# Moving VectorE's gate/up subtraction one tile ahead in a sparse-expert stage

## The chip, the cores and the metric

One core of a Trainium2 chip. The metric is the device time of one execution in microseconds, the median of the runs shown; lower is better.

## The reference

Four sequences of 2048 tokens of width 512 pass through two residual layers. The first is a selective state-space layer (layer norm, convolution over 4 taps, projection, scan, output projection). The second, where the change lies, is a mixture of 64 experts with 8 chosen per token, cut here to what matters:

```python
idx_flat = topk_idx.reshape(-1)
sort = jnp.argsort(idx_flat)
x_sorted = x_flat[sort // TOPK]
g = jax.lax.ragged_dot(x_sorted, we_gate, group_sizes)
u = jax.lax.ragged_dot(x_sorted, we_up, group_sizes)
o = jax.lax.ragged_dot(jax.nn.silu(g) * u, we_down, group_sizes)
y = jnp.zeros_like(x_flat).at[sort // TOPK].add(o * w_sorted[:, None])
```

Gate and up are 512x256 per expert, down is 256x512, all in float32. 8192 tokens times 8 experts are 65536 rows.

## The kernel before

The program runs in stages: the state-space layer's inputs, its scan, a pass over token blocks (router, shared expert), a table of tiles, and last `expert_tiles`, which is about four fifths of the time and the only stage that the change touches. It works on 576 tiles of up to 128 rows, sorted by expert. A float32 product is made as three products of numbers cut to a high and a low part: high times high, high of x times low of w, low of x times high of w.

Five engines each walk the tiles in an order written out by hand, and wait for each other on semaphores only.

- **SyncE** (`load_weights`, lines 1480 to 1491) runs six tiles ahead: it waits until the subtraction of the down part of an earlier tile has freed a half of `w_raw` (`w_low_ready[1]`), then issues gate, up and down, on the condition that the tile's weights are new. `w_raw` has two halves, `w_high` and `w_low` have four slots each. `retire` waits for an add to `out` to land.
- **GpSimd** gathers x of the tile five ahead (L1518) and adds the result of the tile two behind to `out` (L1526), the latter only when the tiles that it shares tokens with are retired.
- **TensorE**, step i: turns x of tile i+1 (`turn_x`, L1562), which waits until VectorE has taken x of tile i; at i = 1 modulo 4 searches the next four tiles' tokens (`find`, L1574); gate/up of tile i (L1592, twelve products into one PSUM bank), with register reads between the products (`read_ahead`, line 1624, most of them at i = 0 modulo 4); turns h of tile i-1 (L1621); down of tile i-2 (L1611). `turn_h` waits for VectorE's low part of the h before it.
- **ScalarE**, step i: takes the high part of x of tile i+1 (L1678), copies ids and weight, casts the high part of new gate/up weights for tile **i+2** (`split_high` part 0, L1670) and of new down weights for tile i+1 (part 1), silu of tile i (L1689), high part of h of tile i-1 (L1694).
- **VectorE**, step i (`step`, lines 1784 to 1800): reads register words of the tiles that it will need (`words.load`, whose instructions have line 1446), takes the low part of x of tile i+1 (`keep_low`, L1741, the "take"), subtracts new gate/up weights of tile i+1 (`split_low` part 0, L1733), subtracts new down weights of tile i (part 1, L1733 too), at i = 2 and 3 modulo 4 picks tokens (`pick`, L1772 to L1781), at i = 2 modulo 4 marks (`mark`, L1765), makes silu times up of tile i (`hidden`, L1753, the inner product's input), takes the low part of h of tile i-1 (`keep_h_low`, L1747) and scales the output of tile i-2 (`scale`, L1760).

`split_low` waits for ScalarE's cast of that part, branches on whether the tile's weights are new, and in either case drains the engine and counts up. Its queue runs in order, so what stands behind a wait or a drain waits as well. VectorE's loop holds four steps; because registers don't pass from one turn of the loop to the next in the program's text, the step at i = 0 modulo 4 loads the words that the other steps have from their forerunners.

Of the kernel before, what the change touches and what calls it, by code (L numbers as in the profile page):

```python
# [33 lines left out]
UNROLL, SHORT = 8, 4  # L34
# [7 lines left out]
def after(eng, sem, count):  # L42

    if not isinstance(count, int) or count > 0:
        eng.wait_ge(sem, count)
# [1297 lines left out]
def expert_tiles(nc, k):  # L1343
# [8 lines left out]
    with ExitStack() as ctx:  # L1352
# [89 lines left out]
        def exists(i):  # L1442
            return not isinstance(i, int) or 0 <= i < TILES
# [26 lines left out]
        def split_weights(eng, words, s, move):  # L1470

            half = eng.snap(words.place(s) & 1)
            with eng.If(words.is_new(s)):
                move(half, words.place(s))
# [252 lines left out]
        def _(v):  # L1727
            words = Words(v)

            def split_low(i, s, part):  # L1730
                v.wait_ge(w_high_ready[part], i + 1)
                v.sem_inc(dve_begun, 1)
                split_weights(v, words, s, lambda half, place: nc.vector.tensor_tensor(  # L1733
                    w_low[:, bass.ds(place, 1), PARTS[part]], w_raw[:, bass.ds(half, 1), PARTS[part]],
                    w_high[:, bass.ds(place, 1), PARTS[part]].bitcast(F32), ALU.subtract))
                v.drain().then_inc(w_low_ready[part], 1)  # L1736

            def keep_low(i, s):
                v.wait_ge(xT_high_ready, i + 1)
                after(v, gu_done, i - 1)  # L1740
                nc.vector.tensor_tensor(xT_low[:, s % 2], ps_x[:], xT_high[:, s % 2].bitcast(F32),  # L1741
                                        ALU.subtract).then_inc(xT_low_ready, 1)

            def keep_h_low(i, s):
                v.wait_ge(hT_high_ready, i + 1)
                after(v, y_done, i - 1)
                nc.vector.tensor_tensor(hT_low[:, s % 2], ps_h[:], hT_high[:, s % 2].bitcast(F32),  # L1747
                                        ALU.subtract).then_inc(hT_low_ready, 1)

            def hidden(i, s):  # L1750
                v.wait_ge(silu_ready, i + 1)
                after(v, ht_done, i - 1)
                nc.vector.tensor_tensor(h[:, s % 2, :], silu[:, s % 2, :], ps_gu[s % 2][:, 1, :],  # L1753
                                        ALU.mult).then_inc(h_made, 1)

            def scale(i, s, slot):
                v.wait_ge(y_done, i + 1)
                v.wait_ge(weight_ready, i + 1)
                after(v, retired, i - YS + 2)
                nc.vector.tensor_scalar(y[:, bass.ds(slot, 1), :].rearrange("p o d -> p (o d)"), ps_y[s % 2][:],  # L1760
                                        weight[:, bass.ds(slot, 1)], None, ALU.mult).then_inc(y_made, 1)

            def mark(i):

                nc.vector.tensor_tensor(past[:], k.slot_row[:].unsqueeze(1).to_broadcast([NB, SHORT, P]),  # L1765
                                        k.begin[:, bass.ds(i, SHORT)].unsqueeze(2).to_broadcast([NB, SHORT, P]),
                                        ALU.is_ge).then_inc(marked, SHORT)

            def pick(i, t):

                v.wait_ge(found, i + t + 2)
                nc.vector.tensor_tensor(rest[:, t:t + 2], k.rank[:, bass.ds(i + t, 2)], ps_find[t // 2][:, :, P],  # L1772
                                        ALU.subtract)
                v.drain()
                for u in range(2):
                    nc.vector.scalar_tensor_tensor(out=below[:, u], in0=ps_find[t // 2][:, u, 0:P],  # L1776
                                                   scalar=rest[:, t + u:t + u + 1], in1=k.last_weight[:],
                                                   op0=ALU.is_le, op1=ALU.mult,
                                                   accum_out=tokens[:, t + u:t + u + 1])
                v.drain()  # L1780
                nc.vector.tensor_tensor(tile_ids[:, bass.ds(i + t, 2)], tokens[:, t:t + 2], ps_find[t // 2][:, :, P + 1],  # L1781
                                        ALU.add).then_inc(picked, 2)

            def step(i, s, slot):
                if s == 0:
                    words.load(i, s)
                words.load(i + 1, (s + 1) % SHORT)
                if exists(i + 1):
                    keep_low(i + 1, (s + 1) % SHORT)
                    split_low(i + 1, (s + 1) % SHORT, 0)  # L1790
                split_low(i, s, 1)
                if s in (2, 3) and exists(i - s + AHEAD_FIND):
                    pick(i - s + AHEAD_FIND, 2 * s - 4)
                if s == 2 and exists(i - s + SHORT + AHEAD_FIND):
                    mark(i - s + SHORT + AHEAD_FIND)
                hidden(i, s)
                if exists(i - 1):
                    keep_h_low(i - 1, (s - 1) % SHORT)
                if exists(i - 2):
                    scale(i - 2, (s - 2) % SHORT, slot(UNROLL - 2))  # L1800
# [4 lines left out]
                pick(i, 0)  # L1805
                pick(i, 2)
            mark(AHEAD_FIND)
            words.load(0, 0)
            split_low(0, 0, 0)
            keep_low(0, 0)  # L1810
            short_walk(v, step)
            keep_h_low(TILES - 1, SHORT - 1)
            for i in (2, 1):
# [103 lines left out]
```

## Time and profile before

| what | value |
|---|---|
| median of 3 runs | 3840.3 us (3835.18 to 3843.41) |
| the profiled execution | 3837.43 us |
| its span | 3835.7 us |
| TensorE busy with matmuls | 3532.6 us (92%) |
| VectorE busy | 2327.1 us (61%) |
| ScalarE busy | 1360.8 us (35%) |
| GpSimd busy | 1736.8 us (45%) |
| mean granted TensorE clock | 0.971 of full speed |

Times of the profile are counted from the first instruction. A busy share is that of the engine's own work: register, branch, semaphore and drain instructions are not in it, though they take their time in the engine's queue. L and a number is a line of the kernel; "<-" behind an idle time names what ended it, and "issue" stands for nothing that the profile shows, often the engine's own queue.

### The profile page before, as it was taken

The numbers are of one execution on the slowest core, as the hardware profiler recorded it, in microseconds if no ns is written. First come the engines' busy times: TensorE is split into PE (matmuls) and PEld (weight loads), VectorE is DVE, ScalarE is ACT, GpSimd is POOL, SyncE is SP. The second block draws the span as 40 slices with busy tenths as digits, with TensorE's granted clock in tenths as the row PEclk, the third lists the DMA queues.
The fourth block names the chain that finished last, engine by engine and source line by source line (L and its number), as shares of the span: only waits on it lengthen the run. The fifth ranks groups of instructions, "written<-read, shape, count | busy, mean of one in ns | idle before, by whom it ended". The sixth has DMA issues, their size and how long they took to land.

```text
span 3835.7 us, 109938 instructions
## 1 busy us (share of the span) xinstructions
PE 3532.6 (92%) x17240; PEld 2862.0 (75%) x17241; DVE 2327.1 (61%) x5877; ACT 1360.8 (35%) x4103; POOL 1736.8 (45%) x1372
## 2 busy tenths in 40 slices
PE   5929988769999999999999999999999999999996
PEld 3517777648787788787888788888887878888885
DVE  5457777655656566666565656566556566566653
ACT  2233333223334333343333433333333343333331
POOL 1011111125555555555555555555555555555543
PEclk9969999879999999999999999999999999999998
DMA  3323333336667666676666766666666667667654
GB/s 125 104 80 110 120 111 109 81 81 127 154 141 170 140 156 124 141 171 157 126 123 130 185 114 139 142 143 138 127 143 123 140 155 174 138 127 168 129 99 74
DMA packets 217551, 502.59 MB, mean 131 GB/s; under 512 B 47504, under 2 KB 47632, under 8 KB 217114
## 3 DMA queue, kind: packets, MB, share of 16 engines
q0 software_dynamic: 129024, 320.94, 43.4%
q1 hardware_dynamic: 87130, 176.22, 13.9%
q10 hardware_dynamic: 1344, 4.85, 0.4%
q8 instruction: 18, 0.29, 0.0%
q14 instruction: 35, 0.29, 0.0%
HBM read 1115.79 MB, written 191.41 MB: 341 GB/s over the span
## 4 chain that ended last, share of the span: by engine, by line
PE 67%; issue 4%; DMA 3%; DVE 2%; DVEq 1%; ACT 1%; ACTq 0%; POOLq 0%; SPq 0%; POOL 0%
PE e_ps_gu L1592 38%; PE e_ps_y L1611 19%; PE e_ps_x L1562 6%; PE e_ps_h L1621 3%; DMA out<-e_y,e_y_ids 3%; PE e_ps_find L1574 1%; DVE e_w_low L1733 1%; DVEq L1446 1%; DMA e_w_raw<-in_L_ffn_we_down 0%; DVE e_below L1776 0%; ACT e_w_high L1670 0%; DVE e_xT_low L1741 0%; DVEq L1736 0%; ACT e_xT_high L1678 0%; DVE e_y L1760 0%
## 5 line engine op out<-in xcount | busy, mean ns | idle before, releaser
L1526 POOL DMA_INDIRECT out<-e_y,e_y_ids x576 | 994.4, 1726 | 1231.8 <-SPq L1496 601.9
L1592 PE MATMUL e_ps_gu<-e_w_high,e_xT_high 128*128 x2304 | 689.0, 419 | 31.2 <-issue 25.8
L1518 POOL DMA_INDIRECT e_x<-token_rows,e_x_ids x576 | 619.7, 1076 | 212.8 <-issue 169.9
L1592 PE MATMUL e_ps_gu<-e_w_high,e_xT_low 128*128 x2304 | 636.2, 398 | 0.0
L1592 PE MATMUL e_ps_gu<-e_w_low,e_xT_high 128*128 x2304 | 635.7, 398 | 0.0
L1689 ACT ACTIVATE e_silu<-e_ps_gu 128x256 f32<-128x256 f32 x576 | 222.2, 386 | 1018.7 <-PE e_ps_gu L1592 994.2
L1760 DVE TENSOR_SCALAR e_y<-e_ps_y,e_weight 128x512 f32 (+1 forms) x576 | 430.0, 746 | 236.2 <-PE e_ps_y L1611 223.6
L1741 DVE TENSOR_TENSOR e_xT_low<-e_ps_x,e_xT_high 128x512 fp32r<-128x512 f32 x576 | 397.2, 690 | 265.1 <-ACT e_xT_high L1678 126.8
L1592 PEld LDWEIGHTS e_ps_gu<-e_w_high,e_xT_low 128*128 128x128 f32 x2304 | 436.1, 189 | 107.1
L1592 PEld LDWEIGHTS e_ps_gu<-e_w_low,e_xT_high 128*128 128x128 f32 x2304 | 435.2, 189 | 102.6
L1592 PEld LDWEIGHTS e_ps_gu<-e_w_high,e_xT_high 128*128 128x128 f32 x2304 | 396.9, 192 | 111.3 <-issue 48.9
L1753 DVE TENSOR_TENSOR e_h<-e_silu,e_ps_gu 128x256 f32<-128x256 f32 x576 | 240.1, 417 | 384.7 <-ACT e_silu L1689 348.5
L1678 ACT CAST e_xT_high<-e_ps_x 128x512 fp32r<-128x512 f32 x576 | 337.0, 585 | 336.8 <-PE e_ps_x L1562 335.7
L1562 PEld LDWEIGHTS e_ps_x<-ident,e_x 128*128 128x128 f32 x2304 | 365.3, 204 | 66.4 <-DVE e_xT_low L1741 10.3
L1611 PE MATMUL e_ps_y<-e_w_high,e_hT_high 128*128 x1152 | 412.3, 438 | 0.0
L1562 PE MATMUL e_ps_x<-ident,e_x 128*128 128x128 f32 x2304 | 367.6, 282 | 12.1 <-DVE e_xT_low L1741 10.0
L1611 PE MATMUL e_ps_y<-e_w_high,e_hT_low 128*128 x1152 | 363.0, 396 | 0.0
L1611 PE MATMUL e_ps_y<-e_w_low,e_hT_high 128*128 x1152 | 362.8, 396 | 0.0
L1698 ACT CAST e_x_ids<-e_tile_ids (+1 forms) x576 | 110.1, 192 | 499.3 <-issue 382.8
L1621 PEld LDWEIGHTS e_ps_h<-ident,e_h 128*128 128x128 f32 x1152 | 225.4, 197 | 58.2 <-DVE e_h L1753 8.7
L1611 PEld LDWEIGHTS e_ps_y<-e_w_high,e_hT_low 128*128 128x128 f32 x1152 | 218.4, 190 | 51.1
L1611 PEld LDWEIGHTS e_ps_y<-e_w_low,e_hT_high 128*128 128x128 f32 x1152 | 216.7, 188 | 52.7
(292 smaller groups left out, 4140.4 us busy)
## 6 DMA issues: line engine op xcount, KB each, us to landing
e_w_raw<-in_L_ffn_we_gate SPq DMA_DIRECT2D x576, 512.0 KB
e_w_raw<-in_L_ffn_we_up SPq DMA_DIRECT2D x576, 512.0 KB
e_w_raw<-in_L_ffn_we_down SPq DMA_DIRECT2D x576, 512.0 KB
a_x<-in_L_attn_x SPq DMA_DIRECT2D x64, 256.0 KB, 3.8
t_x_in<-in_L_attn_x SPq DMA_DIRECT2D x64, 256.0 KB, 2.7
token_rows<-t_xn SPq DMA_DIRECT2D x64, 256.0 KB, 2.0
out<-t_y_out SPq DMA_DIRECT2D x64, 256.0 KB, 2.1
e_x<-token_rows,e_x_ids POOLq DMA_INDIRECT x576
```

The source lines that it names most:

```text
L1518: pool.indirect_dma_start(x[:, s % XS, :], None, k.rows, bass.IndirectOffsetOnAxis(x_ids[:, s:s + 1], 0)) \
L1526: pool.indirect_dma_start(k.out, bass.IndirectOffsetOnAxis(y_ids[:, s:s + 1], 0), y[:, s % YS, :], None, compute_op=ALU.add).then_inc(adde ...
L1562: last = nc.tensor.transpose(ps_x[:, c, :], chunks[:, c, :], k.ident[:])
L1592: last = nc.tensor.matmul(ps_gu[s % 2][:], x[:, s % 2, c, :], w[:, c], start=(n == 0), stop=(n == 3 * DC - 1))
L1611: last = nc.tensor.matmul(ps_y[s % 2][:], x[:, s % 2, c, :], w[:, c], start=(n == 0), stop=(n == 3 * FC - 1))
L1621: last = nc.tensor.transpose(ps_h[:, c, :], chunks[:, c, :], k.ident[:])
L1678: nc.scalar.copy(xT_high[:, s % 2], ps_x[:]).then_inc(xT_high_ready, 1)
L1689: nc.scalar.activation(silu[:, s % 2, :], ps_gu[s % 2][:, 0, :], ACT.Silu).then_inc(silu_ready, 1)
L1698: nc.scalar.copy(x_ids[:, bass.ds(column, 1)], tile_ids[:, bass.ds(i, 1)]).then_inc(ids_ready, 1)
L1741: nc.vector.tensor_tensor(xT_low[:, s % 2], ps_x[:], xT_high[:, s % 2].bitcast(F32), ALU.subtract).then_inc(xT_low_ready, 1)
L1753: nc.vector.tensor_tensor(h[:, s % 2, :], silu[:, s % 2, :], ps_gu[s % 2][:, 1, :], ALU.mult).then_inc(h_made, 1)
L1760: nc.vector.tensor_scalar(y[:, bass.ds(slot, 1), :].rearrange("p o d -> p (o d)"), ps_y[s % 2][:], weight[:, bass.ds(slot, 1)], None, ALU. ...
```

## The change

In VectorE's walk the subtraction of new gate/up weights is made for tile i+2 instead of i+1, and stands behind the subtraction of the down part, the picks and the mark, directly in front of the inner product. The register words are loaded for i+2 in every step, and at i = 0 modulo 4 for i and i+1 as well. In front of the loop, the subtraction is made for tiles 0 and 1.

```diff
             def step(i, s, slot):
                 if s == 0:
                     words.load(i, s)
-                words.load(i + 1, (s + 1) % SHORT)
+                    words.load(i + 1, s + 1)
+                words.load(i + 2, (s + 2) % SHORT)
                 if exists(i + 1):
                     keep_low(i + 1, (s + 1) % SHORT)
-                    split_low(i + 1, (s + 1) % SHORT, 0)
                 split_low(i, s, 1)
                 if s in (2, 3) and exists(i - s + AHEAD_FIND):
                     pick(i - s + AHEAD_FIND, 2 * s - 4)
                 if s == 2 and exists(i - s + SHORT + AHEAD_FIND):
                     mark(i - s + SHORT + AHEAD_FIND)
+                if exists(i + 2):
+                    split_low(i + 2, (s + 2) % SHORT, 0)
                 hidden(i, s)
...
             mark(AHEAD_FIND)
-            words.load(0, 0)
-            split_low(0, 0, 0)
+            for i in range(2):
+                words.load(i, i)
+                split_low(i, i, 0)
             keep_low(0, 0)
             short_walk(v, step)
```

## Rows read from the trace of the kernel before

**Rows 1.** The page: its first line, and the chain that ended last, by line.

```profile
span 3835.7 us, 109938 instructions
...
PE e_ps_gu L1592 38%; PE e_ps_y L1611 19%; PE e_ps_x L1562 6%; PE e_ps_h L1621 3%; DMA out<-e_y,e_y_ids 3%; PE e_ps_find L1574 1%; DVE e_w_low L1733 1%; DVEq L1446 1%; DMA e_w_raw<-in_L_ffn_we_down 0%; DVE e_below L1776 0%; ACT e_w_high L1670 0%; DVE e_xT_low L1741 0%; DVEq L1736 0%; ACT e_xT_high L1678 0%; DVE e_y L1760 0%
```

**Rows 2.** Timeline, first gate/up products of tiles 0, 229, 233, 540: start us, us, what.

```profile
812.96 1.63 PE L1592 MATMUL e_ps_gu<-e_w_high,e_xT_high 128*128 x3
...
2000.87 0.97 PE L1592 MATMUL e_ps_gu<-e_w_high,e_xT_high 128*128 x3
...
2021.06 1.20 PE L1592 MATMUL e_ps_gu<-e_w_high,e_xT_high 128*128 x4
...
3615.13 1.17 PE L1592 MATMUL e_ps_gu<-e_w_high,e_xT_high 128*128 x4
```

**Rows 3.** Chain of waits in order of time, from tile 542's output: start, us, what.

```profile
3648.02 4.83 DMA out<-e_y,e_y_ids
```

**Rows 4.** Instructions of line 1733: count, duration ns (min/median/max), first and last start.

```profile
L1733 DVE TENSOR_TENSOR e_w_low<-e_w_raw,e_w_high x128: 1224/1749/2349, 809.0 to 3608.4; - x128
```

**Rows 5.** Quiet step of tile 52: timeline, and line 1446 in that step and in all.

```profile
1079.22 1.17 PE L1592 MATMUL e_ps_gu<-e_w_high,e_xT_high 128*128 x4
...
1081.30 0.69 DVE L1741 TENSOR_TENSOR e_xT_low<-e_ps_x,e_xT_high 128x512 fp32r<-128x512 f32 x1 [1.27 <-ACT e_xT_high L1678]
1081.49 1.91 ACT L1670 CAST e_w_high<-e_w_raw  x1 [0.44 <-issue]
...
1084.64 0.73 PE L1592 MATMUL e_ps_gu<-e_w_high,e_xT_high 128*128 x2
...
L1446 DVEq TENSOR_LOAD <-tiles x2: 308/310/311, 1079.8 to 1080.5; - x2
...
L1446 DVEq TENSOR_LOAD <-tiles x720: 300/311/1152, 807.4 to 3787.0; - x180
```

**Rows 6.** Timeline: step of tile 108.

```profile
1372.87 1.17 PE L1592 MATMUL e_ps_gu<-e_w_high,e_xT_high 128*128 x4
...
1375.70 0.69 DVE L1741 TENSOR_TENSOR e_xT_low<-e_ps_x,e_xT_high 128x512 fp32r<-128x512 f32 x1 [1.06 <-issue]
...
1378.30 0.96 PE L1592 MATMUL e_ps_gu<-e_w_high,e_xT_high 128*128 x3
```

**Rows 7.** Timeline: step of tile 60, which has new weights.

```profile
1121.21 1.17 PE L1592 MATMUL e_ps_gu<-e_w_high,e_xT_high 128*128 x4
...
1124.51 0.69 DVE L1741 TENSOR_TENSOR e_xT_low<-e_ps_x,e_xT_high 128x512 fp32r<-128x512 f32 x1 [1.05 <-PE e_ps_gu L1592]
...
1127.11 1.20 PE L1592 MATMUL e_ps_gu<-e_w_high,e_xT_high 128*128 x4 [0.21 <-ACT e_xT_high L1678]
```

**Rows 8.** Timeline: steps of tile 43, which has new weights, and 44.

```profile
1032.29 1.17 PE L1592 MATMUL e_ps_gu<-e_w_high,e_xT_high 128*128 x4
...
1035.22 0.67 DVE L1741 TENSOR_TENSOR e_xT_low<-e_ps_x,e_xT_high 128x512 fp32r<-128x512 f32 x1
...
1037.21 1.17 PE L1592 MATMUL e_ps_gu<-e_w_high,e_xT_high 128*128 x4
...
1041.68 0.69 DVE L1741 TENSOR_TENSOR e_xT_low<-e_ps_x,e_xT_high 128x512 fp32r<-128x512 f32 x1 [1.05 <-issue]
...
1044.26 1.19 PE L1592 MATMUL e_ps_gu<-e_w_high,e_xT_high 128*128 x4 [0.21 <-issue]
```

**Rows 9.** Timeline: steps of tiles 303 and 304, behind new tile 302.

```profile
2392.00 0.41 DVE L1747 TENSOR_TENSOR e_hT_low<-e_ps_h,e_hT_high 128x256 fp32r<-128x256 f32 x1
...
2395.14 0.94 PE L1592 MATMUL e_ps_gu<-e_w_high,e_xT_high 128*128 x3
...
2397.47 0.49 PE L1592 MATMUL e_ps_gu<-e_w_high,e_xT_high 128*128 x1 [1.39 <-issue]
```

**Rows 10.** Timeline: issue and first use of the weights of tile 257.

```profile
2135.17 0.35 SPq L1489 DMA_DIRECT2D e_w_raw<-in_L_ffn_we_gate  x1
...
2145.09 1.90 ACT L1670 CAST e_w_high<-e_w_raw  x1 [11.50 <-DMA e_w_raw<-in_L_ffn_we_down]
```

## The prediction

> **What bounds the kernel now.** I read the page first, then the chain of waits in order of time, then the timeline of single tiles. The chain runs over TensorE in nearly all of the expert stage [rows 1]; what is to be seen is that it is the matmuls' own time, so another engine costs something only where it makes TensorE late. Call the tile number modulo 4 its position. From the first gate/up product of a tile at position 1 to the same product four tiles on is 20.19 us when nothing disturbs (2021.06 less 2000.87) [rows 2]. From tile 0 (812.96) to tile 540 (3615.13) are 2802.2 us; 135 times 20.19 are 2725.6. So **77 us are stalls**, and that is all this change could win. From tile 542 on the add to `out` sets the pace, each waiting for the one before it to retire [rows 3]; nothing new is loaded there, so what is won or lost before it moves the end one for one.
>
> Where are the 77 us? There are 64 experts with new weights, hence 128 subtractions of 2.3 (gate/up) or 1.23 us (down) [rows 4]. I numbered each by the count of L1741 before it and compared the distance between successive first products with its quiet value (5.42 us out of position 0, 4.91 to 4.94 out of the others). All the excess lies within three tiles of a new expert. By the position of the new tile: position 3 (17 of them) 1.6 us each; position 2, 18 of them, of which the 11 that are 6 modulo 8 pay 1.1 to 1.6 and the other 7 pay 0 to 0.5; position 0 (19, tile 0 among them) about 0.75; position 1 (10) about 0.15. These make 60; the other 17 are clumps of new tiles, 13 of them at tiles 254 to 257.
>
> **The mechanism, from three timelines.** VectorE's take of x for the next tile (L1741) must end before TensorE can turn the tile after that. The critical step is position 0, where VectorE's queue has the loop's branch and two register loads in front of that take. In a quiet step the take ends 2.77 us after the tile's first product (1081.30+0.69-1079.22) [rows 5]. At tile 108 it ends at 3.52 and the next tile comes after 5.43 us: no loss [rows 6]. At tile 60 (new) it ends at 3.99 and the next comes after 5.90: loss 0.48 [rows 7]. At tile 44 (behind new tile 43) it ends at 5.16 and the next comes after 7.05: loss 1.63 [rows 8]. So the loss is **the take's end less 3.52**, one for one. The reason is TensorE's own queue: it stands at the turn until the take is in, and has the search's register work behind it.
>
> **Part 1, what is added: one more register load at position 0.** The step loaded the words of i and i+1 there; now i, i+1 and i+2. The other steps load one, as before. Two loads stand 0.75 us apart (1079.8 and 1080.5, rounded; 0.31 of it the load, the rest register work) [rows 5], and the take waits for the queue, not for ScalarE, in such a step. So the quiet take moves from 2.77 to 3.52: exactly to the knee. Typical steps lose nothing, but there is no cover left. The load takes 0.30 to 1.15 us, median 0.31 [rows 5]; counted over those 720 records, four in five take at most 0.33, the mean is 0.37, and the distance between the two loads of a step has a mean of 0.84. Where an old load is slow the quiet take is at 2.8 to 3.4 already (a quarter of the steps). Lower bound 0, upper bound 0.84 less the slack for every one. I take 0.13 us for each of some 75 quiet steps: **+10 us**; the bounds are +3 and +25.
> The Trainium skill (DMA: Bandwidth & Descriptors, section Latency and other measured facts) gives a floor of about 600 ns for a tensor_load. The trace has 310 ns at the median, so the measurement decides; by the page's figure the added load would be some 1.04 us, an estimate, and the loss 0.3 us in each of 134 steps, +40 us.
>
> **Part 2, what is moved: the 2.3 us subtraction goes from step j-1 to step j-2, behind pick and mark.** It is free of ScalarE's timing: the cast for the tile two ahead starts 0.19 us after the take does and takes 1.91 [rows 5], and at positions 2 and 3 the pick fills that time; at positions 0 and 1 VectorE waits up to 0.9 us for it, where it would have waited for silu anyway. The drain now also waits for mark; 0.1 us, inside the wait for silu. The inner product is up to 2.5 us later in step j-2; TensorE turns it a whole tile later, so that is covered. By position of the new tile j, with the take's end after the first product as the measure:
> - Position 3. Before, both parts fell in the two steps with picks: the take of step j ended at 3.60 (1035.22+0.67-1032.29), that of the next at 5.16 [rows 8]. After, the first part falls in position 1, which has no pick; I put the take of step j at 1.9 instead of 3.6, so the next at 3.5, plus 0.75 and 0.1 for slow loads: 4.3, a loss of 0.8 where it was 1.63. 16 times -0.85: **-14 us**.
> - Position 2. The second part now meets a VectorE that is 0.6 us less late. For the 11 with j=6 modulo 8 the loss has another place: TensorE's queue waits for VectorE's hT_low (2392.00), 2 us later than in a quiet step, and then has loop branch and register loads to do; it shows as 1.39 us in the middle of the gate/up product [rows 9]. I take 0.6 instead of 1.35: **-8 us**. The other 7 stay: 0.
> - Position 1. Its first part was in position 0, where it cost nothing; now it is in position 3 with a pick, which is what position 0 had before [rows 7]: take at about 4.05, with the load 4.8, a loss of 1.3 to 1.4. 9 times 1.25: **+11 us**.
> - Position 0. First part in position 2, with pick and mark, then a step to catch up: 5.16 less 1.5 (the second part and its queue time) plus 0.75 is 4.4, a loss of 0.9 against 0.5 to 0.6, nine times; for the multiples of 8 the register loads of TensorE join in, 1.3 against 0.87, eight times: **+7 us**.
> - The clump at 254 to 257. The second subtraction of 254 no longer stands behind 2.29 us for 255, so SyncE's issue at 2135.17 and the cast that waited 11.50 us for the weights [rows 10] come up to 2.5 us earlier; but the subtraction for 257 now stands in front of the inner product of 255. **-2 us**. Slow loads in the steps near new tiles: **+3 us**.
>
> **Sum.** 10 -14 -8 +11 +7 -2 +3 = +7 us. The profiled execution took 3837.4 us (its span of 3835.7 [rows 1] and 1.7 around it), so 3844 by its own time. The median of the three runs, 3840.3, is 2.9 higher; against it the forecast is **3847 us**.
>
> **Rivals.**
> 1. *Slower, 3866 us.* The added load is the mechanism, at position 0: from a take's end of 3.52 on, all of it is paid in 134 steps. If it costs 0.95 us rather than 0.75 (a slow load pushes the next, or the third waits behind VectorE's full queue), it costs another 0.15 to 0.2 in each, some +20 to +25, on top of the forecast or in place of its gains. For it: the quiet sum lands exactly on the knee, and loads up to 1.15 us exist. Against it: four loads in five are within 0.02 of 0.31. It decides from 0.1 us of additional load on. The Trainium skill's figure above is this rival's extreme.
> 2. *Faster, 3813 us.* Apart by a step, the two subtractions no longer add up, and the steps at positions 2, 3 and 0 catch up to their quiet times: 17 of position 3 win 1.5, 11 of position 2 win 1.3, the clumps half of 17; that is -48, against +10 and +11. For it: most of the 77 us come from two parts in neighbouring steps. Against it: the part that moves lands in a pick step for 29 of 64.
> 3. *No difference, 3840 us.* The losses come from TensorE's own register work, which the change leaves alone, and a late take only coincides. Against it: three tiles fall on one line within 0.01 us.
>
> **How the numbers follow.** A measurement of this kernel can tell 0.2% (7.7 us). The forecast has 0.55 (3838 to 3858; of that 0.28 is within 0.2%), rival 1 has 0.17, rival 2 has 0.17, rival 3 has 0.11. So slower 0.27+0.17, same 0.28+0.11, faster 0.17. The range reaches from half of rival 2 to rival 1's price: 3820 to 3867, with the bounds of part 1 inside.
>
> **What the profile after would show.** Right: register loads on VectorE 864 instead of 720; at a quiet tile like 52 the take ends 3.5 us after the first product and the next product still comes after 5.42 to 5.5; tile 44's distance falls from 7.05 to about 6.2; tiles 188 or 312, in front of new tiles at position 1, rise by over a microsecond. Wrong: if quiet distances out of position 0 grow by over 0.2 us, rival 1 holds; if tile 44's distance falls to 5.5, rival 2; if tiles 40, 44 and 304 stay as they are, rival 3.

## The result, and the profile after

The changed kernel takes **3856.95 us** (median of 6 runs, 3855.76 to 3859.46), the kernel before beside it 3838.6 us (6 runs, 3835.18 to 3843.41). The ratio is 1.0048 [1.0035, 1.0061]: slower by 18 us. The forecast was 3847 us in a range of 3820 to 3867, with slower as its likeliest sign. So the sign and the range hold, and the size is off: +7 us were forecast. The kernel before was measured at 3838.6 us here and at 3840.3 us when the forecast was made.

The page after, its first line, the chain by engine and by line, and the group of the takes (busy us, mean ns, idle before it and what ended it):

```profile
span 3855.1 us, 110654 instructions
...
PE 61%; DVE 4%; issue 4%; DVEq 4%; DMA 3%; ACT 1%; ACTq 1%; SPq 0%; POOLq 0%; POOL 0%
PE e_ps_gu L1592 34%; PE e_ps_y L1611 16%; PE e_ps_x L1562 6%; DMA out<-e_y,e_y_ids 3%; PE e_ps_h L1621 3%; DVE e_w_low L1733 2%; DVEq L1446 2%; PE e_ps_find L1574 1%; ACT e_w_high L1670 1%; DMA e_w_raw<-in_L_ffn_we_down 1%; DVE e_below L1776 1%; DVEq L1736 0%; DVE e_xT_low L1741 0%; DVE e_y L1760 0%; DVEq L1733 0%
...
L1741 DVE TENSOR_TENSOR e_xT_low<-e_ps_x,e_xT_high 128x512 fp32r<-128x512 f32 x576 | 397.9, 691 | 325.5 <-issue 251.1 <-PE e_ps_gu L1592 25.5 <-ACT e_xT_high L1678 23.6
```

Against [rows 1], the register loads (L1446 on VectorE's queue) went from 1% to 2% of the chain. The same group of takes before the change stood idle for 265.1 us, of which ScalarE ended 126.8 and "issue" 90.1. That VectorE's takes used to wait for ScalarE doesn't follow from it. At tile 52 before the change ScalarE's part of x ended at 1080.81 and the take began at 1081.30, so VectorE's own queue already held it for 0.49 us; after the change the two stand at 1083.23 and 1084.42, 1.19 us apart. So what ended an idle time by the row isn't always what came last: the queue's own register work is not among the things that it can name.

The first gate/up products of tiles 0, 229, 233 and 540, in the timeline after:

```profile
815.44 2.05 PE L1592 MATMUL e_ps_gu<-e_w_high,e_xT_high 128*128 x4
...
2007.64 1.20 PE L1592 MATMUL e_ps_gu<-e_w_high,e_xT_high 128*128 x4
...
2027.83 0.97 PE L1592 MATMUL e_ps_gu<-e_w_high,e_xT_high 128*128 x3
...
3633.49 1.17 PE L1592 MATMUL e_ps_gu<-e_w_high,e_xT_high 128*128 x4
```

Four quiet tiles still take 20.19 us, as in [rows 2]. From tile 0 to tile 540 are 2818.0 us, where it was 2802.2. The span grew by 19.4 us: 2.5 before tile 0, 15.9 up to tile 540, 1.0 behind it. The stalls up to tile 540 grew from 76.8 to 92.7 us, so they are the larger part of it.

The 2.5 us ahead of tile 0 are of two kinds. The first subtraction and the first take, before the change and after:

```profile
808.96 2.29 DVE L1733 TENSOR_TENSOR e_w_low<-e_w_raw,e_w_high  x1 [0.86 <-ACTq L1672]
811.37 0.69 DVE L1741 TENSOR_TENSOR e_xT_low<-e_ps_x,e_xT_high 128x512 fp32r<-128x512 f32 x1
```

```profile
810.31 2.29 DVE L1733 TENSOR_TENSOR e_w_low<-e_w_raw,e_w_high  x1 [0.87 <-issue]
813.85 0.69 DVE L1741 TENSOR_TENSOR e_xT_low<-e_ps_x,e_xT_high 128x512 fp32r<-128x512 f32 x1 [1.25 <-issue]
```

1.35 us were there before the changed code began: the first mark of the stage already came 1.34 us later. Over the 14 profiled executions, whose code up to there is the same on VectorE, that mark stands anywhere from 794.9 to 799.3 us, so 1.35 us is no effect of the change that these traces can tell. The other 1.1 are what now stands between the first subtraction and the first take: the load for tile 1 with the wait, branch and drain of its subtraction. I had not counted it. The first take starts 3.54 to 3.56 us after the first subtraction in the eight executions that have this code, and 2.41 to 2.42 us in five of the six that don't (3.21 in e10).

**The quiet step.** Tile 52, to be read against [rows 5]: its timeline, and line 1446 on VectorE's queue in that step (count, ns min/median/max, first and last start) and in all:

```profile
1081.69 1.17 PE L1592 MATMUL e_ps_gu<-e_w_high,e_xT_high 128*128 x4
...
1084.42 0.69 DVE L1741 TENSOR_TENSOR e_xT_low<-e_ps_x,e_xT_high 128x512 fp32r<-128x512 f32 x1 [1.92 <-issue]
...
1086.78 0.40 PE L1574 MATMUL e_ps_find<-ranks,e_past 64*128 x4
...
1087.10 1.20 PE L1592 MATMUL e_ps_gu<-e_w_high,e_xT_high 128*128 x4
```

```profile
L1446 DVEq TENSOR_LOAD <-tiles x3: 301/301/313, 1082.2 to 1083.7; - x3
```

```profile
L1446 DVEq TENSOR_LOAD <-tiles x864: 298/305/1005, 808.7 to 3801.5; - x173
```

Three loads stand about 0.75 us apart, and there are 864 in all, 144 more. The take ends 3.42 us after the product (1084.42+0.69-1081.69), 0.65 later than before, and the next product still comes after 5.41. The knee of [rows 6] is real too: over all position-0 steps after the change the next product is on time (within 0.01 us) up to a take's end of 3.52. The 52 quiet steps of position 0 lost 0.7 us together.

**In front of a new tile at position 1.** Tiles 187 to 189 after the change; 189 has new weights:

```profile
1790.28 1.91 ACT L1670 CAST e_w_high<-e_w_raw  x1 [0.17 <-issue]
1792.88 2.29 DVE L1733 TENSOR_TENSOR e_w_low<-e_w_raw,e_w_high  x1 [0.80 <-ACTq L1672]
...
1793.98 1.17 PE L1592 MATMUL e_ps_gu<-e_w_high,e_xT_high 128*128 x4
...
1798.50 0.69 DVE L1741 TENSOR_TENSOR e_xT_low<-e_ps_x,e_xT_high 128x512 fp32r<-128x512 f32 x1 [1.72 <-issue]
...
1799.25 0.75 PE L1562 MATMUL e_ps_x<-ident,e_x 128*128 128x128 f32 x4 [0.59 <-DVE e_xT_low L1741]
1799.93 0.96 PE L1574 MATMUL e_ps_find<-ranks,e_past 64*128 x4
...
1801.10 1.78 PE L1592 MATMUL e_ps_gu<-e_w_high,e_xT_high 128*128 x4 [0.21 <-issue]
...
1807.57 0.71 PE L1592 MATMUL e_ps_gu<-e_w_high,e_xT_high 128*128 x2
```

This shows the whole loss. The subtraction waits 0.80 us for the cast, then holds the rest of step 187 back. The branch and three loads come on top (1.72 idle), and the take ends at 5.21 us (1799.19 less 1793.98). The next product comes after 7.12 instead of 5.42: a loss of 1.70, and 5.21 less 3.52 is 1.69. Before, this distance was quiet. And then tile 189 itself takes 6.47 us instead of 4.94, with nobody late. The granted clock says why (columns: stretch, us, TensorE's busy us, clock, DMA share, GB/s):

```profile
1800.00:1801.00 1.00, 0.66 (x4) 1.00 0.49 53
1801.00:1802.00 1.00, 0.90 (x3) 0.72 0.95 175
1802.00:1803.00 1.00, 1.00 (x4) 0.50 0.90 241
1803.00:1804.00 1.00, 1.00 (x4) 0.50 0.14 55
1804.00:1805.00 1.00, 1.00 (x4) 0.57 0.88 43
1805.00:1806.00 1.00, 1.00 (x7) 1.00 0.66 102
```

For some 3.4 us TensorE ran at 0.50, its level of 1.2 GHz, behind the stall, and lost another 1.53 us. Tiles 313 and 341 had the same stall (1.71 and 1.69 us) and no half clock.

Why the knee lies there can be seen in the search. In the quiet step above its four matmuls take 0.40 us: their register instructions start between 1085.4 and 1086.5, behind the take's end at 1085.11 and ahead of the matmuls at 1086.78, while TensorE still works on what stands in front of them. At tile 188 the take's end is at 1799.19, the register instructions start between 1799.5 and 1800.6, and the four matmuls, from 1799.93 on, take 0.96 us because they wait for them one by one.

**Behind a new tile at position 3.** Tile 44, against [rows 8], with what delayed it, two steps earlier:

```profile
1016.55 0.35 SPq L1489 DMA_DIRECT2D e_w_raw<-in_L_ffn_we_gate  x1
...
1026.12 1.91 ACT L1670 CAST e_w_high<-e_w_raw  x1 [1.43 <-DMA e_w_raw<-in_L_ffn_we_down]
1028.71 2.29 DVE L1733 TENSOR_TENSOR e_w_low<-e_w_raw,e_w_high  x1 [2.51 <-ACTq L1672]
...
1039.75 1.17 PE L1592 MATMUL e_ps_gu<-e_w_high,e_xT_high 128*128 x4
...
1046.74 1.20 PE L1592 MATMUL e_ps_gu<-e_w_high,e_xT_high 128*128 x4 [0.21 <-issue]
```

The distance is 6.99 us, where 6.2 was forecast and 7.05 was before. Here the weights came late: SyncE issued them at 1016.55, before the change at 1011.77. Of these 4.8 us, 2.5 are the later start of tile 44's step, so 2.2 us are left; why they came later I have not followed. The cast waited 1.43 us for them and the subtraction 2.51 for the cast. Tile 43 is not the usual case: of the six isolated new tiles at position 3, five have their weights in time, and there the subtraction still waits 2.01 us for the cast, the take of the step of the new tile ends at 2.59 to 2.80 and the next one at 4.57 to 4.80. Tile 304, the other one I had named, went from 7.06 to 6.23. All subtractions together now wait 63.3 us for ScalarE's queue, in 40 places, where it was 1.7 us in 2.

**By position.** A loss is the distance of two successive first products less its quiet value, summed from three tiles ahead of a new tile to three behind it. The table has the means over the 31 new tiles that have no other within four tiles (the isolated ones), by number modulo 8. The last two columns are the sum around all other new tiles but tile 0 (clumps) and the stalls from tile 0 to tile 540. The columns don't add up to the last one: where two new tiles are five or six tiles apart, a distance between them counts for both. In column 3 that matters: it holds the losses of tiles 214 and 486 as well, 1.07 and 1.06 us before and 0.26 each after. Without them it is 1.62 before, 1.45 after and 0.60 in e2.

| kernel | 0 | 4 | 1 | 5 | 2 | 6 | 3 | 7 | clumps | stalls |
|---|---|---|---|---|---|---|---|---|---|---|
| (tiles) | 4 | 6 | 3 | 2 | 5 | 5 | 4 | 2 | | |
| before | 0.67 | 0.53 | 0.11 | 0.18 | 0.47 | 1.53 | 2.15 | 1.82 | 51.8 | 76.8 |
| after | 1.80 | 1.26 | 2.74 | 2.45 | 0.29 | 0.60 | 1.58 | 1.25 | 53.0 | 92.7 |
| e1_load_only | 1.64 | 1.20 | 0.84 | 0.81 | 1.03 | 1.50 | 3.94 | 2.20 | 63.9 | 108.0 |
| e2_load_at_1 | 1.78 | 0.52 | 1.03 | 0.96 | 0.48 | 1.41 | 0.85 | 0.50 | 47.3 | 73.3 |
| e4_after_take_first | 3.12 | 0.00 | 0.00 | 0.00 | 0.39 | 1.01 | 0.27 | 0.03 | 35.5 | 53.8 |
| e5_before_take_first | 1.39 | 0.54 | 1.96 | 1.35 | 0.19 | 1.47 | 1.49 | 2.02 | 47.5 | 79.9 |
| e6_behind_take | 4.44 | 3.51 | 3.77 | 3.24 | 1.09 | 1.62 | 2.56 | 1.89 | 88.8 | 168.2 |
| e7_mixed | 1.20 | 1.15 | 0.79 | 0.87 | 0.35 | 0.34 | 1.04 | 0.83 | 48.6 | 75.2 |
| e8_behind_h | 1.20 | 0.37 | 0.83 | 0.76 | 0.84 | 1.31 | 0.87 | 0.55 | 50.4 | 75.5 |
| e9_after_find_first | 2.09 | 0.00 | 0.43 | 0.39 | 0.33 | 0.63 | 0.37 | 0.57 | 42.6 | 58.7 |
| e10_before_find_first | 0.66 | 0.00 | 0.04 | 0.24 | 0.18 | 1.63 | 0.89 | 1.80 | 36.6 | 53.6 |
| e11_take_first_mark_3 | 1.92 | 0.00 | 0.20 | 0.19 | 0.28 | 0.73 | 0.23 | 0.23 | 38.1 | 51.7 |
| e12_all | 2.31 | 0.00 | 0.18 | 0.04 | 0.25 | 0.78 | 0.25 | 0.77 | 40.8 | 56.1 |

For all new tiles, clumps included, each distance can be put down to the last new tile up to three tiles before it or, where there is none, to the next one. Then every distance from tile 4 to tile 540 counts once (us, by position of the new tile):

| kernel | 0 | 1 | 2 | 3 | quiet steps |
|---|---|---|---|---|---|
| before | 15.1 | 4.7 | 17.2 | 41.0 | -0.1 |
| after | 28.7 | 18.2 | 10.1 | 36.7 | 0.7 |
| e1_load_only | 26.0 | 11.1 | 18.8 | 53.5 | 0.5 |

### The profile page after: what moved, and what is told of

Read it like the earlier page. It is cut to its first block, busy times and chain, and to the rows that moved or that the text cites. A ratio compares the mean times of both kernels' runs of the same rounds, so it can differ in the third digit from the quotient of the medians.

```text
span 3855.1 us, 110654 instructions
## 1 busy us (share of the span) xinstructions
PE 3542.6 (92%) x17240; PEld 2861.9 (74%) x17241; DVE 2344.2 (61%) x5877; ACT 1360.5 (35%) x4103; POOL 1654.6 (43%) x1372
## 3 DMA queue, kind: packets, MB, share of 16 engines
q1 hardware_dynamic: 87130, 176.22, 13.6%
## 4 chain that ended last, share of the span: by engine, by line
PE 61%; DVE 4%; issue 4%; DVEq 4%; DMA 3%; ACT 1%; ACTq 1%; SPq 0%; POOLq 0%; POOL 0%
PE e_ps_gu L1592 34%; PE e_ps_y L1611 16%; PE e_ps_x L1562 6%; DMA out<-e_y,e_y_ids 3%; PE e_ps_h L1621 3%; DVE e_w_low L1733 2%; DVEq L1446 2%; PE e_ps_find L1574 1%; ACT e_w_high L1670 1%; DMA e_w_raw<-in_L_ffn_we_down 1%; DVE e_below L1776 1%; DVEq L1736 0%; DVE e_xT_low L1741 0%; DVE e_y L1760 0%; DVEq L1733 0%
## 5 line engine op out<-in xcount | busy, mean ns | idle before, releaser
L1526 POOL DMA_INDIRECT out<-e_y,e_y_ids x576 | 933.2, 1620 | 1332.5 <-SPq L1496 565.3
L1518 POOL DMA_INDIRECT e_x<-token_rows,e_x_ids x576 | 598.8, 1040 | 213.1 <-issue 171.4
L1733 DVE TENSOR_TENSOR e_w_low<-e_w_raw,e_w_high x128 | 226.1, 1766 | 72.4 <-ACTq L1672 63.3
```

What stands on the lines that cost most here:

```text
L1518: pool.indirect_dma_start(x[:, s % XS, :], None, k.rows, bass.IndirectOffsetOnAxis(x_ids[:, s:s + 1], 0)) \
L1526: pool.indirect_dma_start(k.out, bass.IndirectOffsetOnAxis(y_ids[:, s:s + 1], 0), y[:, s % YS, :], None, compute_op=ALU.add).then_inc(adde ...
```

## The experiments

Each was timed against the kernel before on the same chip; those medians were 3834.2 us (e1, e2, e4, e5), 3835.4 (e3, e6, e7, e8) and 3835.4 (the rest). The changed kernel was not timed there again; by its ratio it would take about 3852.5 and 3854 us, and differences to it below are from these two numbers.

**1. Is it the load or the move?** The load alone, in the kernel before, and the changed kernel with its third load moved from position 0 to position 1:

```diff
 e1_load_only (against before)
                 if s == 0:
                     words.load(i, s)
+                    words.load(i + 2, s + 2)
                 words.load(i + 1, (s + 1) % SHORT)
 e2_load_at_1 (against after)
-                if s == 0:
+                if s < 2:
                     words.load(i, s)
-                    words.load(i + 1, s + 1)
                 words.load(i + 2, (s + 2) % SHORT)
```

> The kernel before, with only the third register load at position 0 (its words are used by nothing). Theory (loss at position 0 is the take's end less 3.52 us): the quiet take ends near 3.4 instead of 2.77 and quiet steps lose nothing; behind new tiles each take that was already over the knee is 0.67 us later, for 17 + 18 + about 10 of the 64 new tiles: +25 to +32 us, 3864 to 3871. Rival (the moved subtraction itself costs, the load is free): 3838 to 3842.

> The changed kernel, with the third load put from position 0 to position 1, where the take has over 2 us to spare. Theory: the quiet take of position 0 is back near 2.7, every loss behind a take over the knee is 0.67 us smaller: about 45 of them, -25 to -33 us, 3824 to 3832, so faster than both. Rival (the move costs by the later inner product): within 3 us of the change, 3854 to 3860.

e1: 3869.5 us, ratio 1.009 [1.0073, 1.0107], as expected. e2: 3835.6 us, 1.0004 [0.9994, 1.0013]. The load alone costs 35 us, in no quiet step (0.5 us in all) and beside new tiles: 12.5 us at position 3, 10.9 at 0, 6.4 at 1 and 1.6 at 2. New tiles that are 6 modulo 8 pay nothing (1.53 and 1.50). A part of it is the clock: up to tile 540 TensorE stood at 0.50 for 30.7 us in e1 and 17.1 before, which at 1.53 us for each 3.4 is an estimated 6 of the 31 us of added stalls.

The changed kernel has the same three loads as e1 and is 17 us ahead of it (3852.5 to 3869.5). So the 18 us of the change are two effects: the load costs 35, and the move, with the load where it is, gives 17 back. By the second table the move saves 17 us of stalls at position 3 and 9 at position 2, and loses 10 at positions 0 and 1. With the load moved to position 1 (e2), the move costs nothing and gains nothing in the sum: it takes 1.0 to 1.3 us from each new tile of position 3 and gives 0.8 to 1.1 back at 0, 1 and 5 modulo 8. e2 came out 4 to 12 us above what I expected of it. Its stalls fell by 19 us instead of 25 to 33: out of position 0 by 21.6, and the distances out of positions 1 and 2 grew by 2.7 together, against the changed kernel. No run tells whether that is the load at position 1.

**2. Two loads more.**

```diff
 e3_two_loads (against before)
                     words.load(i, s)
+                    words.load(i + 2, s + 2)
+                    words.load(i + 3, s + 3)
                 words.load(i + 1, (s + 1) % SHORT)
```

> The kernel before with two further register loads at position 0 whose words nothing uses (four in all). Theory (knee at 3.52 us): the quiet take ends near 4.10, 0.58 over the knee, so every quiet step out of position 0 is 0.58 us longer, 5.42 to 6.0, and losses behind new tiles grow by 1.3: 3940 to 3965 in all. Rival (a register load costs its own 0.7 us or nothing wherever it stands, no knee): proportional to the first load's 35 us, 3900 to 3910.

One execution alone: 3968.1 us, just above what was expected. The quiet step of tile 52 in its timeline:

```profile
1089.90 1.17 PE L1592 MATMUL e_ps_gu<-e_w_high,e_xT_high 128*128 x4
...
1093.36 0.69 DVE L1741 TENSOR_TENSOR e_xT_low<-e_ps_x,e_xT_high 128x512 fp32r<-128x512 f32 x1 [2.66 <-PE e_ps_gu L1592]
...
1095.95 0.49 PE L1592 MATMUL e_ps_gu<-e_w_high,e_xT_high 128*128 x1 [0.21 <-issue]
```

The take ends at 4.15, which is 0.63 beyond 3.52, and the next product comes after 6.05, a loss of 0.63. Now the quiet steps pay as well, 33.8 us. So the first added load filled the cover, and of the second almost all is paid: the quiet take moved from 3.43 to 4.15.

**3. The take in front of the loads**, which takes the loads out of its way:

```diff
 e4_after_take_first (against after); e5_before_take_first (against before) likewise
             def step(i, s, slot):
+                if exists(i + 1):
+                    keep_low(i + 1, (s + 1) % SHORT)
                 if s == 0:
...
-                if exists(i + 1):
-                    keep_low(i + 1, (s + 1) % SHORT)
```

> The changed kernel, with the take of x in front of the register loads in each step, so that the take waits for no load. Theory: the quiet take of position 0 ends when ScalarE's part lets it, near 2.3 us; the losses behind new tiles at position 0 shrink by 1.1 us or more, those in the middle of the gate/up product at 6 and 0 modulo 8 stay in part: stalls of 93 us fall to 25 to 45, 3790 to 3810. Rival (the loads only move from in front of the take to in front of the subtractions and the inner product, and TensorE then waits for h instead): 3845 to 3857.

> The kernel before with the same edit, the take in front of the register loads. Theory: the knee at position 0 is cleared for most new tiles: stalls of 77 us fall to 25 to 40, 3790 to 3805; beside the changed kernel with this edit it tells what the move is worth once the loads are out of the way (theory: within 8 us of it). Rival: 3832 to 3840.

e4: 3818.3 us, 0.9954 [0.9938, 0.9971]. e5: 3843.1 us, 1.0023 [1.0012, 1.0034]. e4 gained 16 us and was expected at 3790 to 3810: its stalls fell to 53.8 us and not to 25 to 45, because new tiles at 0 modulo 8 went from 1.80 to 3.12 (half clock at two of the four, tiles 16 and 496, is an estimated 0.77 of it). In the step of tile 188 the loads are out of the take's way: its end is at 3.52, on the knee, and the next product comes after 5.42.

```profile
1784.30 1.17 PE L1592 MATMUL e_ps_gu<-e_w_high,e_xT_high 128*128 x4
...
1787.14 0.68 DVE L1741 TENSOR_TENSOR e_xT_low<-e_ps_x,e_xT_high 128x512 fp32r<-128x512 f32 x1
...
1789.72 0.50 PE L1592 MATMUL e_ps_gu<-e_w_high,e_xT_high 128*128 x1
```

For e5 my theory fell: I expected as large a gain. Its takes are early too (2.96 us here), but the loads now stand in front of the subtraction for the very next tile, and the next product comes after 7.06 us:

```profile
1785.34 1.17 PE L1592 MATMUL e_ps_gu<-e_w_high,e_xT_high 128*128 x4
1787.61 0.69 DVE L1741 TENSOR_TENSOR e_xT_low<-e_ps_x,e_xT_high 128x512 fp32r<-128x512 f32 x1 [1.46 <-ACT e_xT_high L1678]
...
1789.74 2.29 DVE L1733 TENSOR_TENSOR e_w_low<-e_w_raw,e_w_high  x1 [1.44 <-issue]
1792.40 0.95 PE L1592 MATMUL e_ps_gu<-e_w_high,e_xT_high 128*128 x3 [1.57 <-DVEq L1736]
```

TensorE waits for w_low itself, 17.8 us in 13 places of e5 by its waits. In e4 the subtractions wait longer for ScalarE's queue than in the changed kernel (96.5 us to 63.3), but TensorE is nowhere seen to wait for w_low. With the take first, the moved kernel is 25 us ahead of the unmoved one (3818.3 to 3843.1), where I had expected the two within 8 us.

**4. Other places for the subtraction.** Directly behind the take; in the old place for positions 0 and 1 and in the new one for positions 2 and 3; and, in e4, behind the low part of h:

```diff
 e6_behind_take (against after)
                     keep_low(i + 1, (s + 1) % SHORT)
+                if exists(i + 2):
+                    split_low(i + 2, (s + 2) % SHORT, 0)
                 split_low(i, s, 1)
...
-                if exists(i + 2):
-                    split_low(i + 2, (s + 2) % SHORT, 0)
                 hidden(i, s)
 e7_mixed (against after; in front of the loop as in the kernel before)
                     keep_low(i + 1, (s + 1) % SHORT)
+                if s in (3, 0) and exists(i + 1):
+                    split_low(i + 1, (s + 1) % SHORT, 0)
                 split_low(i, s, 1)
...
-                if exists(i + 2):
+                if s in (0, 1) and exists(i + 2):
                     split_low(i + 2, (s + 2) % SHORT, 0)
 e8_behind_h (against e4)
-                if exists(i + 2):
-                    split_low(i + 2, (s + 2) % SHORT, 0)
                 hidden(i, s)
                 if exists(i - 1):
                     keep_h_low(i - 1, (s - 1) % SHORT)
+                if exists(i + 2):
+                    split_low(i + 2, (s + 2) % SHORT, 0)
```

> The changed kernel with the subtraction for the tile two ahead directly behind the take, in front of the down part, pick and mark, instead of behind them. Theory: VectorE's queue now waits 1 to 2 us for ScalarE's cast of that part with pick and mark behind the wait, so new tiles at positions 0 and 1, whose subtraction falls in a step with a pick, lose 1 to 1.5 us more each: 15 to 30 us over the change, which stands at about 3852 on this chip. Rival (place within the step is nothing, the work is the same): 3848 to 3856.

> The changed kernel with the subtraction one tile ahead at its new place only for new tiles at positions 2 and 3; for positions 0 and 1 it stands as before, for the next tile, behind the take. Three loads at position 0 as in the change. Theory: losses of position 1 fall from 2.4 to 2.7 to the 0.8 that they have with the third load alone, position 0 stays (1.2 and 1.7), positions 2 and 3 keep what the change gave them: 13 to 20 us under the change, 3832 to 3840. Rival (the move as a whole, not its position, makes the cost): half way to the kernel with the load alone, 3855 to 3862.

> The changed kernel with the take in front of the loads, and with the subtraction for the tile two ahead behind the inner product and the low part of h instead of in front of them. Theory: what is left of the stalls there (1.1 to 1.7 us behind each new tile that is 0 modulo 8, in the middle of the gate/up product) comes from the late low part of h and goes; those of 6 modulo 8 stay: stalls of 54 us fall to about 40, 3802 to 3810. Rival (they come from TensorE's own register loads): no change, 3815 to 3820, or slower by the later scaling of y.

e6: 3935.5 us, 1.0263 [1.0246, 1.028], some 82 us above the changed kernel, well over twice what I expected at most. Its subtractions wait 116.6 us for ScalarE with down part, picks and inner product behind them. In front of tile 189:

```profile
1816.40 2.29 DVE L1733 TENSOR_TENSOR e_w_low<-e_w_raw,e_w_high  x1 [2.23 <-ACTq L1672]
...
1817.49 1.17 PE L1592 MATMUL e_ps_gu<-e_w_high,e_xT_high 128*128 x4
...
1823.58 0.69 DVE L1741 TENSOR_TENSOR e_xT_low<-e_ps_x,e_xT_high 128x512 fp32r<-128x512 f32 x1 [1.70 <-issue]
...
1826.17 1.19 PE L1592 MATMUL e_ps_gu<-e_w_high,e_xT_high 128*128 x4 [0.21 <-issue]
```

The wait grew from 0.80 to 2.23 us, the take ends at 6.78 and the loss is 3.26. So the place behind the picks was right for a subtraction that must wait for its cast.

e7: 3841.1 us, 1.0011 [1.0001, 1.0021]: just above the 3832 to 3840 expected, 13 us under the changed kernel. Position 1 falls from 2.74 and 2.45 to 0.8 and 0.9, as expected.

e8: 3838.4 us, 1.0012 [1.0002, 1.0022], where 3802 to 3810 was expected. It cures most of the loss at 0 modulo 8 (1.20 for 3.12), but 0.3 to 0.8 us are added at each of the others and the clumps go from 35.5 to 50.4 us. The likely reason is that in e4 the subtraction fills VectorE's wait for silu, and here it doesn't; no run tests that alone.

**5. TensorE's side: the search in front of the turn.** The knee is TensorE's queue: behind the turn it has the search's register work before it can start the next product. If the search goes first, a late take should hurt less.

```diff
 e9_after_find_first (against after); e10_before_find_first (against before) the same
-                if exists(i + 1):
-                    turn_x(i + 1, (s + 1) % UNROLL)
                 if s % SHORT == 1 and exists(i - 1 + AHEAD_FIND):
                     find(i - 1 + AHEAD_FIND, held)
+                if exists(i + 1):
+                    turn_x(i + 1, (s + 1) % UNROLL)
```

> The changed kernel with one edit on TensorE: at position 1 the search for tokens is issued in front of the turn of x instead of behind it, so its register work no longer stands behind TensorE's wait for the take. Theory (the knee at 3.52 us is that register work, not the turn itself, which TensorE's matmuls reach only some 4.3 us after the tile's first product): the knee moves to about 4.3, new tiles at positions 1, 3 and 0 (4 modulo 8) lose 0.5 us or less, what shows in the middle of the gate/up product at 6 and 0 modulo 8 stays: stalls of 93 us fall to 45 to 60, 3810 to 3825. Rival (the turn needs the take at that time anyway): 3848 to 3856.

> The kernel before with the same edit on TensorE. Theory: the loss of 1.63 us behind position 3 falls to 0.8 (take at 5.16, knee at 4.3), that of 4 modulo 8 (take at 4.06) goes, 6 modulo 8 stays at 1.1 to 1.6: stalls of 77 us fall to 50 to 60, 3810 to 3822. Beside the run with this edit on the changed kernel it tells what the change is worth when the third load has cover: within 8 us of each other. Rival: 3832 to 3839.

e9: 3820.1 us, 0.9963 [0.9949, 0.9977]. e10: 3815.0 us, 0.9947 [0.993, 0.9964]. Both times as expected. The step of tile 188 in e9:

```profile
1784.27 1.17 PE L1592 MATMUL e_ps_gu<-e_w_high,e_xT_high 128*128 x4
...
1788.85 0.69 DVE L1741 TENSOR_TENSOR e_xT_low<-e_ps_x,e_xT_high 128x512 fp32r<-128x512 f32 x1 [1.72 <-issue]
...
1789.60 0.75 PE L1562 MATMUL e_ps_x<-ident,e_x 128*128 128x128 f32 x4 [0.31 <-DVE e_xT_low L1741]
1790.10 0.48 PE L1592 MATMUL e_ps_gu<-e_w_high,e_xT_high 128*128 x1
```

The take is as late as after the change (5.27 for 5.21), with the same 1.72 us of queue ahead of it. But the product comes 0.56 us behind the take's end instead of 1.91, and the loss is 0.41 (5.83 less 5.42) instead of 1.70. Over all position-0 steps the knee went from 3.52 to about 4.9; I had expected 4.3. The edit leaves VectorE alone, so this isolates the cause of the knee from the cause of the late take. With both kernels cured in this way the changed one is 5 us behind, and the two intervals overlap.

**6. Together.**

```diff
 e11_take_first_mark_3 (against e4)
-                if s == 0:
+                if s < 2:
                     words.load(i, s)
-                    words.load(i + 1, s + 1)
...
-                if s == 2 and exists(i - s + SHORT + AHEAD_FIND):
+                if s == 3 and exists(i - s + SHORT + AHEAD_FIND):
                     mark(i - s + SHORT + AHEAD_FIND)
 e12_all: e11 and the edit of e9
```

> The changed kernel with the take in front of the loads (3818 us where before is 3834), and two more edits: the third load at position 1, and mark at position 3 instead of 2. Theory: what is left there is the late low part of h out of position 2 in front of TensorE's register loads; mark's 0.7 us out of that step takes 0.5 us from each of 19 losses, the load 0.4 us from 7: 3803 to 3811. Rival (mark at position 3 makes the take of position 0 late again): 3818 to 3828.

> All edits together: take in front of the loads, third load at position 1, mark at position 3, search in front of the turn. Theory: nothing is left at position 0, so the search's edit adds little to the run without it: 3798 to 3810. Rival (the search in front delays the turn and ScalarE's part of x by 0.5 us, and that is on the path once VectorE is early): slower than without it, 3812 to 3830.

e11: 3813.7 us, 0.9944 [0.9928, 0.9961], some 3 us above what was expected. e12: 3821.2 us, 0.996 [0.9946, 0.9974], 7.5 us above e11. The rival held for e12: the cures don't add up. That with the takes early there is little beyond the old knee left to save explains why nothing is won; why 4.4 us of stalls come back (most plainly at 0 and 7 modulo 8) no run isolates. **The best are e11 (3813.7) and e10 (3815.0)**, which can't be told apart, 22 and 20 us ahead of the kernel before. Of the two, e10 is a swap of two calls in TensorE's walk and needs nothing of the change.

## Why the prediction was right in sign and short in size

The frame held: stalls of 77 us, the loss as the take's end less 3.52, and the added load as what decides. But the sign owes something to luck. Without the +10 us for quiet steps, which did not come, the same sum gives -3. The measured +18 come from new tiles, where I had put too much gain and too little loss. The measured terms below are from the second table, up to tile 540; the tiles of the clump are in them.

- **Quiet steps, forecast +10, measured below 1.** I put the take at 3.52, exactly on the knee, and charged 0.13 us for slow loads. Its median came to 3.43, and the steps in which it ended later cost 0.7 us together. The cover is 0.1 us thick, as e3 shows, but it was enough. Rival 1 had the right culprit and the wrong place: a load that costs 35 us alone (e1) costs it beside new tiles.
- **Position 3, forecast -14, measured -4.3.** This is the largest miss. The step "I put the take of step j at 1.9 instead of 3.6" failed: where the weights are in time it ended at 2.59 to 2.80, for tile 43 at 3.10. The step at position 1 has no pick, as I said, and so nothing that fills the wait for the cast. I had costed that wait at up to 0.9 us, "where it would have waited for silu anyway"; it is 2.01 us, and the next take ends at 4.57 to 4.80 instead of 4.3.
- **Position 0, forecast +7, measured +13.6.** The mechanism is as put and the size is not: among the isolated tiles 4 modulo 8 was to lose 0.9 and lost 1.26, 0 modulo 8 was to lose 1.3 and lost 1.80.
- **Position 1, forecast +11, measured +13.5.** I put the take at 4.8 and a loss of 1.3 to 1.4. The step that failed is "at positions 2 and 3 the pick fills that time": with 189 new, 0.80 us of waiting for the cast are left behind the pick, the take ends at 5.21 and the loss is 1.70. In 3 of the 5 isolated ones half clock behind the stall adds 1.53, so that these five lose 2.49 us more than before, and no term of mine stood for that. Over the whole stretch the clock matters less: up to tile 540 TensorE stood at 0.50 for 20.5 us, and for 17.1 before, by the same price an estimated 1.5 us of the 16.
- **Position 2, forecast -8, measured -7.1**, nearly all of it at 6 modulo 8, as forecast.
- **The clump at 254 to 257, forecast -2**: 13.1 us became 11.0, -2.1. It is contained in the positions above, as are the slow loads near new tiles, forecast +3.
- **Not foreseen:** the load, branch and drain in front of the first take, +1.1 us.

Rival 2 (faster, the parts no longer add up) is refuted for the change as it stands, and borne out in part for one with the loads behind the take: e4 has position 3 at 0.27 and 0.03, but its stalls fall by 23 us against the kernel before and not by the 48 of the rival. Much of the gain that it described was there, and the queue in front of the take ate it. Rival 3 is refuted by tile 188, which went from quiet to 7.12 us with TensorE's code untouched; half of it was true all the same, as e10 shows: TensorE's register work sets how early the take has to be.

## What to carry to other kernels

Work that is moved to an earlier step brings its operands' register loads with it; count where these land on the in-order queue, and try the handover that others wait for in front of them. Try it and don't assume it: it won 34 us in the changed kernel (e4) and lost 9 in the kernel before (e5), where the loads came to stand in front of something needed just as soon. A step that ends exactly on its knee is safe alone, and dear wherever a second delay meets it. And look on the waiting engine for what is queued behind its wait: moving that ahead of the wait can be worth as much as making the awaited thing earlier, and here it took one swap.

## What the runs showed of the hardware

- **A stall of TensorE can be paid twice, and it needn't be one long idle time.** Behind a loss of 1.7 us came some 3.4 us at 0.50 of its clock, another 1.53 us, at tiles 189, 385 and 441 after the change, and not at 313 and 341, which had the same loss. The longest idle time of its matmuls in that stall is 0.59 us. Beside the one with which the expert stage begins, it has six such stretches up to tile 540 after the change and three before it. One of those before lasts 10.2 us, behind the wait for weights of [rows 10]; this is its start, in the kernel before (columns as above):

```profile
2146.00:2148.00 2.00, 0.00 (x0) 1.00 0.00 0
2148.00:2150.00 2.00, 1.11 (x3) 0.58 0.00 0
2150.00:2152.00 2.00, 2.00 (x6) 0.50 0.00 0
```

- **What a register load on VectorE's queue costs depends on what stands behind it**: 0.30 us in the record, about 0.75 us in the queue with its register work, and 35 us of the kernel's time for 144 of them (e1), next to nothing of it in quiet steps.
- **Register work behind a wait doesn't overlap it.** The product came 1.91 us after the take with the search behind the turn, and 0.56 with the search ahead (after and e9, tile 188). Behind the wait the search's four matmuls took 0.96 us, in a quiet step 0.40.
